# Similarity blocks by symmetry: products on and right of the diagonal, turned copies left of it, three PSUM pairs, and four margins on GpSimd

## The chip, the core and the metric

The kernel runs on one core of a Trainium2 chip. The metric is device time in microseconds (us) of one execution; a kernel's time is the median of several. The engines are TensorE (PE; its weight loads are shown as PEld), VectorE (DVE), ScalarE (ACT), GpSimd (POOL) and SyncE (SP), which issues all DMAs here. Each engine runs its own list of instructions in order, and they meet through semaphores.

## The reference

x is 64 batches of 128 x 1024. From it one graph over the 1024 columns is made, and then every batch is mixed along that graph:

```python
h = relu(layernorm(x))                      # over the 1024 columns
x_avg = h.mean over the 64 batches          # a vector of 128 for each of 1024 nodes
x_norm = x_avg / norm(x_avg)
sim = (x_norm @ x_norm.T + 1) * 0.5         # 1024 x 1024, symmetric
adj = (sim + gumbel0 > 1 - sim + gumbel1)   # not symmetric: gumbel is drawn per entry
adj_sym, nmask = clip(adj + adj.T), with the diagonal set
common = nmask @ nmask.T                    # common neighbours
W = adj * common**2 / common.max()          # where valid
Wn = W scaled by deg**-0.5 on both sides
out = x + (Wn.T applied to h @ weight) + bias
```

The comparison comes down to "x_norm @ x_norm.T is greater than gumbel1 - gumbel0"; the right side is called the margin.

## The kernel before

The work has three parts. First, all 64 batches are loaded once and their statistics and the sum of relu(layernorm) are made (to about 107 us of the trace). Second, the graph is made (about 107 to 235 us): norms of the mean's columns, similarity, comparison, symmetrising, counting of common neighbours, degrees, and the scaled matrix split in two f16 parts. Third, batches go in pairs through x·W and the product with the graph's matrix, in a steady loop that TensorE bounds (235 us to the end).

The change is in the second part. N = 1024 is cut into C = 8 block rows of P = 128. PSUM has 8 banks of 128 x 512 fp32, used as four pairs; a pair holds one 128 x 1024 row.

- **Similarity, TensorE (L750 to L762).** For each block row c, two fp32 products of 128x512 (`xn` chunk c against each half of `xn`) go to `ps_sim[c % 2]`, one of two pairs. From row 2 on TensorE waits until comparison c-2 has read its pair (L752). After rows 2 to 5 come two chunks each of batch 1's x·W (`first_xw`, L742), which need only TensorE. The first row also waits for the two halves of `xn` (L1073).
- **Comparison, VectorE (L1076 to L1081).** `margin_of(c)` (L1027) subtracts the two interleaved gumbel planes of block row c, in place, as soon as its 1 MB block is loaded; `margin_of(0)` to `margin_of(3)` stand ahead of the first comparison, the other four between the comparisons. The comparison reads the PSUM pair and the margin and writes 0 or 1 in f16 to `adjm`, and tells it in `s_adj`.
- **ScalarE (L567 to L585).** It makes z of batch 0, relu of batch 1 for TensorE, two y parts, then waits for all of batch 1's x·W (`z_of(0, 0, 1)`, L579), makes two more y parts, and goes on to the masks (L584).
- **GpSimd.** Its last work before the stage are two powers (L393) that make 1/norm; then it waits until the counting stage (L410).
- **Symmetrising, TensorE (L778 to L798).** For block rows 0 and 1, and then 2 to 7, it adds `adjm`, its turned blocks and the identity in PSUM. Rows 0 and 1 go along with the comparisons: `for k in range(C): wait_ge(s_adj, k + 1)`. Row 0 uses `pair[1]`, row 1 `pair[3]`, which ScalarE must have read (`s_z`), since batch 1's x·W was there.
- **SyncE (L294).** When all eight comparisons are done, it issues six loads of x for the first batches (L300) into the space where the last gumbel block was.

Counting (L831 to L852) already uses a symmetry of the same kind, in f16: products on and right of the diagonal, a copy by ScalarE (`copied`, L562), and turned copies as products with the identity (`mirrored`, L846).

Of the kernel before, what the change touches and what calls it, by code (L numbers as in the profile page):

```python
# [23 lines left out]
ALU = mybir.AluOpType  # L24
ACT = mybir.ActivationFunctionType
# [4 lines left out]
P = 128  # L30
# [7 lines left out]
BODY = 8  # L38
RESIDENT = 0
GUMBEL_SLOTS = 7  # L40
EPS = 1e-5
NORM_MIN = 1e-12
TINY = 1e-30
# [8 lines left out]
def gnn_kernel(nc, x, adj, bias, gumbel, out):  # L52
    B, T, N = x.shape
    C = N // P
    H = 512
# [11 lines left out]
    with ExitStack() as ctx:  # L67
        def sb(name, shape, dt=F32):
            return ctx.enter_context(nc.sbuf_tensor(name, shape, dt))

        def sem(name):
            return ctx.enter_context(nc.semaphore(name))


        xring = sb("xring", [P, BODY, N])
# [7 lines left out]
        ident = sb("ident", [P, P])  # L83
# [39 lines left out]
        adjm = xring[:, 0:4, :].bitcast(F16).rearrange("p a (b n) -> p (a b) n", b=2)  # L123
        nmask = xring[:, 4:8, :].bitcast(F16).rearrange("p a (b n) -> p (a b) n", b=2)
        S, sq, xn = (hring[:, k, :] for k in (2, 1, 3))
        x1 = ([xring[:, k, :] for k in range(8)] + [ybuf[:, k, :] for k in range(7)] + [obuf[:, 0, :]])
        gum7 = a16[:, :, :, :, :].bitcast(F32).rearrange("p k m c n -> p (k m c n)").rearrange(
            "p (r n) -> p r n", r=GUMBEL_SLOTS)
        gum = [gum7[:, k, :] for k in range(GUMBEL_SLOTS)] + [
            obuf[:, 2:4, :].rearrange("p a n -> p (a n)")]  # L130
        g0, g1 = ([g.rearrange("p (d g) -> p g d", g=2)[:, k, :] for g in gum] for k in (0, 1))
        margin = g0
        h1 = [hring[:, k, :] for k in range(4)] + [zbuf[:, k, :] for k in (1, 2, 3)] + [obuf[:, 1, :]]
        acc = zbuf[:, 0, :]
        def tile16(half, mat, k):
            return a16[:, half, mat, 2 * k:2 * k + 2, :].rearrange("p c n -> p (c n)")

        masked = [tile16(half, mat, k) for half, mat in ((0, 5), (1, 5), (1, 3), (1, 4)) for k in (0, 1)]
        count16 = [tile16(c // 4, 1 + c // 2 % 2, c % 2) for c in range(C)]
        squares = a16[:, 0, 0, :, :].bitcast(F32).rearrange("p c n -> p (c n)")  # L140
# [16 lines left out]
        pair = [ps[:, 2 * k:2 * k + 2, :].rearrange("p a n -> p (a n)") for k in range(4)]  # L157
# [2 lines left out]
        ps_w = ps[:, 7, :]  # L160
        ps_norm = [ps[:, 6 + half, 0:HC] for half in (0, 1)]
        ps_bc = pair[1]
        ps_sim = [pair[2], pair[0]]
        ps_sym = [pair[1], pair[3], pair[2], pair[0]]
        ps_com = [pair[1], pair[0]]
        ps_diag = pair[2]
# [11 lines left out]
        s_gum = [sem(f"gumbel_loaded{k}") for k in range(C)]  # L178
# [24 lines left out]
        s_bc = sem("rnorm_row_ready")  # L203
        s_xn = sem("xn_ready")
        s_sim = sem("sim_ready")
        s_margin = sem("margin_ready")
        s_adj = sem("adj_ready")
        s_sym = sem("sym_ready")
        s_mask = [sem(f"nmask_ready{k}") for k in (0, 1)]
# [31 lines left out]
        s_xw2 = sem("xw2_ready")  # L241
# [82 lines left out]
        def _(pool):  # L324

            nc.gpsimd.memset(neg_half[:], -0.5).then_inc(s_pchain, 1)
            nc.gpsimd.memset(eps[:], EPS).then_inc(s_pchain, 1)
            nc.gpsimd.memset(minus_one[:], -1.0).then_inc(s_pchain, 1)
# [61 lines left out]
            for half in (0, 1):  # L390
                cols = slice(half * HC, (half + 1) * HC)
                pool.wait_ge(s_n2s, half + 1)
                nc.gpsimd.tensor_tensor(rnorm[:, cols], norm2[:, cols], neg_half[:, cols], ALU.pow).then_inc(s_rn, 1)  # L393

            def z_sums(r):
                pool.wait_ge(s_z, 2 * r + 2)
                pool.wait_ge(s_y, 4 * r + 4)
                nc.gpsimd.tensor_tensor(z[:, 4, :], z[:, 0, :], z[:, 3, :], ALU.add).then_inc(s_zs, 1)  # L398
                pool.wait_ge(s_zs, 4 * r + 1)
                nc.gpsimd.tensor_tensor(z[:, 5, :], z[:, 4, :], z[:, 1, :], ALU.subtract).then_inc(s_zs, 1)  # L400
                nc.gpsimd.tensor_tensor(z[:, 6, :], z[:, 1, :], z[:, 0, :], ALU.subtract).then_inc(s_zs, 1)  # L401
                pool.wait_ge(s_zs, 4 * r + 2)
                nc.gpsimd.tensor_tensor(z[:, 7, :], z[:, 2, :], z[:, 5, :], ALU.subtract).then_inc(s_zs, 1)  # L403
# [12 lines left out]
            with pool.Fori(2, TRIPS * PAIRS) as r:  # L416
                z_sums(r)

        @block.scalar
        def _(act):  # L420
# [69 lines left out]
            def z_of(i, q, b):  # L490

                i, q = i + q // PAIRS, q % PAIRS
                j, r = 2 * q + b, PAIRS * i + q
                if b == 0:
                    act.wait_ge(s_y, 4 * r + 4)
                if isinstance(i, int) and i == 0 and j == EARLY[1]:
                    src = xw_res[:, 0:1, :].rearrange("p a (m n) -> p (a m) n", m=2)
                elif j == RESIDENT:
                    src = xw_res[:, bass.ds(i, 1), :].rearrange("p a (m n) -> p (a m) n", m=2)
                else:  # L500
                    act.wait_ge(s_xw2, (BODY - 1) * i + j + 2)
                    src = ps_xw2.rearrange("p (m n) -> p m n", m=2)
                dst = z[:, 1:3, :] if b == 0 else z[:, 0:4:3, :]
                nc.scalar.activation(dst, src, ACT.Copy, scale=Y_SCALE / W_SCALE).then_inc(s_z, 1)  # L504

            def y_high_first(u):

                act.wait_ge(s_z, 2 if u >= 2 else 1)
                nc.scalar.activation(y16[:, 0, 0, u, :], z[:, (u + 1) % 4, :], ACT.Copy).then_inc(s_yhi, 1)
# [66 lines left out]
            relu_first(1)  # L576
            y_high_first(0)
            y_high_first(1)
            z_of(0, 0, 1)  # L579
            y_high_first(2)  # L580
            y_high_first(3)
# [43 lines left out]
            for n, (mat, rows, k, half) in enumerate(((0, rows_hi, 0, 0), (A12, rows_hi, 0, 1),  # L625
                                                      (1, rows_lo, 1, 0), (2, rows_lo, 1, 1))):
                for part in (0, 1):
                    a, b = 2 * part, 2 * part + 2
# [43 lines left out]
        def _(pe):  # L672
# [8 lines left out]
                             skip_group_check=True).then_inc(s_wsum, 1)  # L681

            for m in range(2):
                nc.tensor.matmul(ps_avg[:, m * H:m * H + P], zeros[:], ones[:], start=True, stop=True,
                                 skip_group_check=True)
# [44 lines left out]
            for half in (0, 1):  # L730
                pe.wait_ge(s_sq, half + 1)
                for k in range(HC):
                    c = half * HC + k
                    mm = nc.tensor.matmul(ps_norm[half][:, k:k + 1], sq[:, c * P:(c + 1) * P], ones[:, 0:1],
                                          start=True, stop=True, skip_group_check=True)
# [6 lines left out]
            def first_xw(j, chunks):  # L742

                pe.wait_ge(s_fh, EARLY.index(j) + 1)
                for c in chunks:
                    mm = nc.tensor.matmul(ps_xw2[:, c * P:(c + 1) * P], first_h[j][:, c * P:(c + 1) * P], w_unit[:],
                                          start=True, stop=True, skip_group_check=True)
                return mm

            for c in range(C):  # L750
                if c >= 2:
                    pe.wait_ge(s_adj, c - 1)  # L752
                for m in range(2):
                    if c == 0:
                        pe.wait_ge(s_xn, m + 1)
                    mm = nc.tensor.matmul(ps_sim[c % 2][:, m * H:(m + 1) * H], xn[:, c * P:(c + 1) * P],  # L756
                                          xn[:, m * H:(m + 1) * H], start=True, stop=True)
                mm.then_inc(s_sim, 1)
                if 2 <= c < 6:
                    mm = first_xw(1, (2 * c - 4, 2 * c - 3))  # L760
                    if c == 5:
                        mm.then_inc(s_xw2, 1)  # L762

            def sym_start(c):

                for m in (LO, HI):
                    nc.tensor.matmul(ps_sym[c % 4][:, m], ident16[:], adjm[:, c, m], start=True, stop=False,
                                     skip_group_check=True)
                nc.tensor.matmul(ps_sym[c % 4][:, c * P:(c + 1) * P], ident16[:], ident16[:],
                                 start=False, stop=False, skip_group_check=True)  # L770

            def sym_part(c, k):

                return nc.tensor.matmul(ps_sym[c % 4][:, k * P:(k + 1) * P], adjm[:, k, c * P:(c + 1) * P], ident16[:],
                                        start=False, stop=True, skip_group_check=True)


            for k in range(C):  # L778
                pe.wait_ge(s_adj, k + 1)
                if k == 1:  # L780
                    pe.wait_ge(s_z, 2)
                if k < 2:
                    sym_start(k)
                if k == 1:
                    sym_part(0, 0)
                    sym_part(1, 0)
                if k >= 1:
                    for c in (0, 1):
                        mm = sym_part(c, k)
                        if k == C - 1:  # L790
                            mm.then_inc(s_sym, 1)
            for c in range(2, C):
# [3 lines left out]
                for k in range(C):  # L796
                    mm = sym_part(c, k)
# [193 lines left out]
        def _(dve):  # L991
# [35 lines left out]
            def margin_of(c):  # L1027

                dve.wait_ge(s_gum[c], 16)
                nc.vector.tensor_tensor(margin[c], g1[c], g0[c], ALU.subtract).then_inc(s_margin, 1)  # L1030
# [43 lines left out]
                                               op0=ALU.mult, op1=ALU.mult).then_inc(s_xn, 1)  # L1074
            margin_of(3)
            for c in range(C):  # L1076
                if c >= 1 and c + 3 < C:
                    margin_of(c + 3)
                dve.wait_ge(s_sim, c + 1)
                dve.wait_ge(s_margin, c + 1)  # L1080
                nc.vector.tensor_tensor(adjm[:, c, :], ps_sim[c % 2], margin[c], ALU.is_gt).then_inc(s_adj, 1)  # L1081

            def y_low_first(u):
                dve.wait_ge(s_yhi, u + 1)
# [277 lines left out]
```

## Time and profile before

| what | us |
|---|---|
| median of 3 runs | 833.32 |
| lowest, highest | 833.02, 834.04 |
| the profiled execution's own time | 834.8 |
| its span, first to last instruction | 833.1 |
| TensorE busy | 808.6 |
| VectorE, ScalarE, GpSimd busy | 573.0, 495.4, 306.0 |
| start of the first similarity product | 114.46 |
| start of the first symmetrising product | 130.45 |

The profile is of one execution; all stamps are from the span's start. Matmuls overlap: each is shown from its start to its modelled end, so the pitch of a series is read from one start to the next, not from the length of one. An fp32 product is shown as two weight loads and two matmul records, an f16 product as one of each.

### The profile page before, as it was taken

The numbers are of one execution on the slowest core, as the hardware profiler recorded it, in microseconds if no ns is written. First come the engines' busy times: TensorE is split into PE (matmuls) and PEld (weight loads), VectorE is DVE, ScalarE is ACT, GpSimd is POOL, SyncE is SP. The second block draws the span as 40 slices with busy tenths as digits, with TensorE's granted clock in tenths as the row PEclk, the third lists the DMA queues.
The fourth block names the chain that finished last, engine by engine and source line by source line (L and its number), as shares of the span: only waits on it lengthen the run. The fifth ranks groups of instructions, "written<-read, shape, count | busy, mean of one in ns | idle before, by whom it ended". The sixth has DMA issues, their size and how long they took to land.

```text
span 833.1 us, 13478 instructions
## 1 busy us (share of the span) xinstructions
PE 808.6 (97%) x4718; PEld 425.4 (51%) x4718; DVE 573.0 (69%) x687; ACT 495.4 (59%) x515; POOL 306.0 (37%) x257
## 2 busy tenths in 40 slices
PE   4999999999999999999999999999999999999997
PEld 3455465754545554555455545554555455545553
DVE  7999998799976656665666566656665666566652
ACT  3888825588566656665566556656665566556631
POOL 4788810300333334333433343333333333333320
PEclk9999999999999999999999999999999999999999
DMA  8999933000842223222222222222222322232111
GB/s 325 409 410 350 420 131 127 27 1 31 315 160 101 101 102 102 101 101 101 101 101 101 101 101 101 101 101 101 101 101 101 113 99 103 101 116 98 51 51 76
DMA packets 30121, 113.14 MB, mean 136 GB/s; under 512 B 3472, under 2 KB 3600, under 8 KB 29072
## 3 DMA queue, kind: packets, MB, share of 16 engines
q1 hardware_dynamic: 30096, 112.80, 36.6%
q8 instruction: 16, 0.26, 0.1%
q14 instruction: 9, 0.07, 0.0%
HBM read 79.23 MB, written 33.55 MB: 135 GB/s over the span
## 4 chain that ended last, share of the span: by engine, by line
PE 81%; issue 5%; DVE 5%; POOL 4%; ACT 2%; DMA 1%; POOLq 0%; ACTq 0%; SPq 0%; DVEq 0%
PE ps L906 64%; PE ps L823 8%; PE ps L922 2%; POOL rstd L350 2%; PE ps L756 2%; PE ps L841 2%; POOL zbuf L360 1%; DVE stats L1001 1%; PE ps L719 1%; DVE ybuf L1122 1%; DMA xring<-in_x_dram 1%; DVE a L1198 1%; ACT zbuf L430 1%; DVE a L1129 0%; POOL nbias L352 0%
## 5 line engine op out<-in xcount | busy, mean ns | idle before, releaser
L906 PE MATMUL ps<-a,ybuf 128*128 128x512 f16 x2604 | 571.2, 379 | 2.9 <-DVE obuf L1271 1.7
L906 PEld LDWEIGHTS ps<-a,ybuf 128*128 128x128 f16 x2604 | 252.2, 98 | 299.1 <-DVE obuf L1271 2.1
L1122 DVE TENSOR_TENSOR ybuf<-zbuf,ybuf 128x1024 f16<-128x1024 f32 x124 | 166.0, 1340 | 155.3 <-ACT ybuf L523 155.3
L398 POOL TENSOR_TENSOR zbuf<-zbuf 128x512 f32<-128x512 f32 x31 | 39.5, 1275 | 426.8 <-ACT zbuf L504 426.8
L523 ACT ACTIVATE ybuf<-zbuf 128x1024 f16<-128x1024 f32 x124 | 117.6, 950 | 112.6 <-POOL zbuf L403 98.6
L541 ACT ACTIVATE obuf<-ps,bias_sb,w_out 128x512 f32<-128x512 f32 x61 | 47.1, 771 | 113.8 <-PE ps L906 111.5
L1111 DVE TENSOR_TENSOR hring<-hring 128x1024 f16<-128x1024 f32 x53 | 65.4, 1234 | 55.9 <-ACT hring L482 55.8
L823 PEld LDWEIGHTS ps<-w,hring 128*128 128x128 f16 x1272 | 75.4, 98 | 12.4 <-issue 0.4
L1281 DVE TENSOR_TENSOR obuf<-obuf,xring 128x1024 f32<-128x1024 f32 x64 | 78.4, 1225 | 2.7
L823 PE MATMUL ps<-w,hring 128*128 128x128 f16 x1272 | 79.7, 219 | 0.3 <-DVE k L1155 0.3
L504 ACT ACTIVATE zbuf<-ps 128x1024 f32<-128x1024 f32 x55 | 56.3, 1023 | 35.0 <-PE ps L823 20.1
L401 POOL TENSOR_TENSOR zbuf<-zbuf 128x512 f32<-128x512 f32 x31 | 68.2, 2199 | 0.0
L403 POOL TENSOR_TENSOR zbuf<-zbuf 128x512 f32<-128x512 f32 x31 | 67.7, 2184 | 0.0
L472 ACT ACTIVATE hring<-xring,nbias,rstd 128x1024 f32<-128x1024 f32 x49 | 60.2, 1228 | 0.6 <-DMA xring<-in_x_dram 0.6
L482 ACT ACTIVATE hring<-xring,nbias,rstd 128x1024 f16<-128x1024 f32 x49 | 60.1, 1227 | 0.0
L400 POOL TENSOR_TENSOR zbuf<-zbuf 128x512 f32<-128x512 f32 x31 | 49.0, 1580 | 2.4
L1001 DVE BATCH_NORM_STATS2 stats<-xring 128x6 f32<-128x512 f32 x64 | 39.2, 673 | 3.1 <-DMA xring<-in_x_dram 2.8
L719 PE MATMUL ps<-hring,ident 128*128 128x512 f32 x76 | 34.4, 599 | 0.3 <-ACT hring L430 0.3
L1001 DVE BATCH_NORM_STATS2 stats<-ybuf 128x6 f32<-128x512 f32 x56 | 34.0, 668 | 0.0
L719 PE MATMUL ps<-zbuf,ident 128*128 128x512 f32 x60 | 29.6, 632 | 3.0 <-ACT zbuf L430 2.8
L541 ACT ACTIVATE p<-ps,bias_sb,w_out 128x512 f32<-128x512 f32 x31 | 24.0, 773 | 10.4 <-PE ps L906 10.4
L1287 DVE SCALAR_TENSOR_TENSOR obuf<-ps,w_out,obuf 128x512 f32<-128x512 f32 x30 | 22.5, 751 | 9.6 <-PE ps L906 9.5
(142 smaller groups left out, 648.7 us busy)
## 6 DMA issues: line engine op xcount, KB each, us to landing
xring<-in_x_dram SPq DMA_DIRECT2D x96, 512.0 KB, 4.4
out_dram<-obuf SPq DMA_DIRECT2D x64, 512.0 KB, 2.9
ybuf<-in_x_dram SPq DMA_DIRECT2D x28, 512.0 KB, 8.6
a<-in_L_gnn_gumbel_dram SPq DMA_DIRECT2D x7, 1024.0 KB, 15.5
obuf<-in_x_dram SPq DMA_DIRECT2D x11, 512.0 KB, 6.9
obuf<-in_L_gnn_gumbel_dram SPq DMA_DIRECT2D x1, 1024.0 KB, 23.6
w<-in_adj_dram SPq DMA_DIRECT2D x1, 64.0 KB, 1.8
bias_sb<-in_L_gnn_bias_dram SPq DMA_DIRECT2D x1, 0.5 KB, 6.8
```

The costliest lines, as they stand in the source:

```text
L401: nc.gpsimd.tensor_tensor(z[:, 6, :], z[:, 1, :], z[:, 0, :], ALU.subtract).then_inc(s_zs, 1)
L403: nc.gpsimd.tensor_tensor(z[:, 7, :], z[:, 2, :], z[:, 5, :], ALU.subtract).then_inc(s_zs, 1)
L472: nc.scalar.activation(h32, src, ACT.Relu, bias=nbias[:, bass.ds(t, 1)], scale=rstd[:, bass.ds(t, 1)]).then_inc(s_h32, 1)
L523: nc.scalar.activation(y16[:, q % 2, 0, a:a + n, :], z[:, a + 1:a + 1 + n, :], ACT.Copy).then_inc(s_yhi, 1)
L541: nc.scalar.activation(dst, src, ACT.Identity, bias=bias_sb[:, 0:1], scale=w_out[:, 0:1]).then_inc(s_v, 1)
L719: mm = nc.tensor.matmul(ps_avg[:, m], ident[:], h[:, m], start=False, stop=True, skip_group_check=True)
L823: mm = nc.tensor.matmul(ps_xw2[:, c * P:(c + 1) * P], h16[b][:, hk, c * P:(c + 1) * P], w16[:, wk, :], start=(hk == wk == 0), stop=(hk == ...
L906: mm = nc.tensor.matmul(bank[q % 2], y16[:, q % 2, yk, u, c * P:(c + 1) * P], a16[:, ak, mat, c, :], start=(start and c == yk == ak == 0), ...
L1001: nc.vector.bn_stats(stats[:, j % 4, 6 * m:6 * m + 6], x1[j][:, m * H:(m + 1) * H]).then_inc(s_bn, 1)
L1111: nc.vector.tensor_tensor(h16[b][:, 1, :], h32, h16[b][:, 0, :], ALU.subtract).then_inc(s_hlo, 1)
L1122: nc.vector.tensor_tensor(y16[:, q % 2, 1, a:a + n, :], z[:, a + 1:a + 1 + n, :], y16[:, q % 2, 0, a:a + n, :], ALU.subtract).then_inc(s_y, 1)
L1281: nc.vector.tensor_tensor(ob, ob, xring[:, j, :], ALU.add).then_inc(s_out, 1)
```

## The change

TensorE makes only the blocks on and right of the diagonal. ScalarE copies the blocks right of the diagonal of each row from PSUM into SBUF in fp32 (`sim_flat`, which lies in `xring[:, 4:8]`, free at that time), and TensorE turns them (a transpose against the identity) into the rows below. A row is told ready (`s_sim`) after its turned blocks; ScalarE's copy of row c waits for that, and TensorE's turned blocks of row c wait for the copy of row c-1. The rows go through three PSUM pairs, so TensorE waits for comparison c-3. The x·W chunks come one row earlier (rows 1 to 4), ahead of the turned blocks. VectorE's comparison waits for the copy of its row too, and the margins of rows 4 to 7 are made by GpSimd after its two powers. The first symmetrising rows wait for six comparisons at least, since row 0's pair is now used by similarity row 5.

```diff
+POOL_MARGINS = 4
+        sim_flat = xring[:, 4:8, :].rearrange("p a n -> p (a n)")
+        sim_start = [sum(C - 1 - m for m in range(k)) * P for k in range(C)]
+        def sim_copy(k, c):
+            a = sim_start[k] + (c - k - 1) * P
+            return sim_flat[:, a:a + P]
-        ps_sim = [pair[2], pair[0]]
+        ps_sim = [pair[2], pair[0], pair[1]]
 # GpSimd, after the two powers
+            for c in range(C - POOL_MARGINS, C):
+                pool.wait_ge(s_gum[c], 16)
+                nc.gpsimd.tensor_tensor(margin[c], g1[c], g0[c], ALU.subtract).then_inc(s_pmargin, 1)
 # ScalarE, after y_high_first(1)
+            for c in range(C - 1):
+                act.wait_ge(s_sim, c + 1)
+                a = sim_start[c]
+                nc.scalar.activation(sim_flat[:, a:a + (C - 1 - c) * P], ps_sim[c % 3][:, (c + 1) * P:],
+                                     ACT.Copy).then_inc(s_simcopy, 1)
 # TensorE
             for c in range(C):
-                if c >= 2:
-                    pe.wait_ge(s_adj, c - 1)
+                if c >= 3:
+                    pe.wait_ge(s_adj, c - 2)
                 for m in range(2):
                     if c == 0:
                         pe.wait_ge(s_xn, m + 1)
-                    mm = nc.tensor.matmul(ps_sim[c % 2][:, m * H:(m + 1) * H], xn[:, c * P:(c + 1) * P],
-                                          xn[:, m * H:(m + 1) * H], start=True, stop=True)
+                    a, b = max(c * P, m * H), (m + 1) * H
+                    if a < b:
+                        mm = nc.tensor.matmul(ps_sim[c % 3][:, a:b], xn[:, c * P:(c + 1) * P], xn[:, a:b],
+                                              start=True, stop=True, skip_group_check=True)
+                if 1 <= c < 5:
+                    last_xw = first_xw(1, (2 * c - 2, 2 * c - 1))
+                    if c == 4:
+                        last_xw.then_inc(s_xw2, 1)
+                if c >= 1:
+                    pe.wait_ge(s_simcopy, c)
+                for k in range(c):
+                    mm = nc.tensor.transpose(ps_sim[c % 3][:, k * P:(k + 1) * P], sim_copy(k, c), ident[:])
                 mm.then_inc(s_sim, 1)
-                if 2 <= c < 6:
-                    mm = first_xw(1, (2 * c - 4, 2 * c - 3))
-                    if c == 5:
-                        mm.then_inc(s_xw2, 1)
             for k in range(C):
-                pe.wait_ge(s_adj, k + 1)
+                pe.wait_ge(s_adj, max(k + 1, 6))
 # VectorE
             for c in range(C):
-                if c >= 1 and c + 3 < C:
-                    margin_of(c + 3)
                 dve.wait_ge(s_sim, c + 1)
-                dve.wait_ge(s_margin, c + 1)
-                nc.vector.tensor_tensor(adjm[:, c, :], ps_sim[c % 2], margin[c], ALU.is_gt).then_inc(s_adj, 1)
+                if c < C - 1:
+                    dve.wait_ge(s_simcopy, c + 1)
+                if c < C - POOL_MARGINS:
+                    dve.wait_ge(s_margin, c + 1)
+                else:
+                    dve.wait_ge(s_pmargin, c + POOL_MARGINS - C + 1)
+                nc.vector.tensor_tensor(adjm[:, c, :], ps_sim[c % 3], margin[c], ALU.is_gt).then_inc(s_adj, 1)
```

## Rows read from the trace of the kernel before

**Rows 1.** The page: busy time, share and instructions of each engine; the chain that ended last.
```profile
PE 808.6 (97%) x4718; PEld 425.4 (51%) x4718; DVE 573.0 (69%) x687; ACT 495.4 (59%) x515; POOL 306.0 (37%) x257
...
PE 81%; issue 5%; DVE 5%; POOL 4%; ACT 2%; DMA 1%; POOLq 0%; ACTq 0%; SPq 0%; DVEq 0%
```

**Rows 2.** Chain of waits, similarity stage, in order of time: start us, us, what.
```profile
119.96 0.44 PE ps L746 x4
...
127.07 3.54 PE ps L756 x8
...
132.97 0.45 PE ps L774 x8
```

**Rows 3.** Groups by line and form, 114 to 132 us: count, busy us, mean ns, idle.
```profile
L1030 DVE TENSOR_TENSOR a<-a 128x1024 f32<-128x1024 f32 x4 | 4.9, 1217 | 0.0
```

**Rows 4.** Timeline of all engines, 113 to 139 us: start us, us, engine, line, instruction.
```profile
113.53 0.69 DVE L1073 SCALAR_TENSOR_TENSOR hring<-hring,ps 128x512 f32<-128x512 f32 x1 [0.98 <-PE ps L695]
...
114.46 5.50 PE L756 MATMUL ps<-hring 128*128 128x512 f32 x12
...
115.40 0.30 PEld L756 LDWEIGHTS ps<-hring 128*128 128x128 f32 x2 [0.75 <-DVE hring L1073]
...
116.57 1.23 DVE L1081 TENSOR_TENSOR xring<-ps,a 128x1024 f16<-128x1024 f32 x1
...
127.11 1.02 ACT L504 ACTIVATE zbuf<-ps 128x1024 f32<-128x1024 f32 x1 [11.86 <-PE ps L746]
...
127.45 0.19 PEld L756 LDWEIGHTS ps<-hring 128*128 128x128 f32 x1 [0.24 <-issue]
...
130.45 0.59 PE L767 MATMUL ps<-xring,ident 128*128 128x512 f16 x2
...
130.65 1.23 DVE L1081 TENSOR_TENSOR xring<-ps,obuf 128x1024 f16<-128x1024 f32 x1 [0.49 <-PE ps L756]
...
131.90 13.90 SPq L300 DMA_DIRECT2D obuf<-in_x_dram  x6
...
138.20 1.23 ACT L472 ACTIVATE hring<-obuf,nbias,rstd 128x1024 f32<-128x1024 f32 x1
```

**Rows 5.** Timeline, TensorE and ScalarE: fp32 records and counts' copies; one line, L802.
```profile
106.57 1.95 PE L705 MATMUL ps<-w_unit,hring 128*128 128x128 f32 x16
...
141.58 0.92 ACT L564 ACTIVATE a<-ps 128x896 f16<-128x896 f32 x1 [1.02 <-PE ps L841]
...
160.34 0.28 ACT L564 ACTIVATE a<-ps 128x128 f16<-128x128 f32 x1 [0.39 <-PE ps L850]
...
L802 PEld LDWEIGHTS ps<-ident,col x2: 79/82/84, 141.2 to 167.4; 128*1 128x1 f32 x2
L802 PE MATMUL ps<-ident,col x2: 270/271/272, 141.4 to 167.4; 128*1 128x128 f32 x2
```

**Rows 6.** Instructions of one line, GpSimd and VectorE: count, ns min/median/max, first and last start.
```profile
110.29 3.12 POOL L393 TENSOR_TENSOR rnorm<-norm,neg_half 128x4 f32<-128x4 f32 x2 [7.96 <-DVE norm L1066]
...
L360 POOL TENSOR_TENSOR zbuf<-zbuf,hring x11: 2357/2366/2378, 15.4 to 91.8; 128x1024 f32<-128x1024 f32 x11
...
L401 POOL TENSOR_TENSOR zbuf<-zbuf x31: 1263/2301/2310, 155.1 to 803.5; 128x512 f32<-128x512 f32 x31
...
L1122 DVE TENSOR_TENSOR ybuf<-zbuf,ybuf x124: 861/1227/2284, 149.1 to 809.1; 128x1024 f16<-128x1024 f32 x93, 128x512 f16<-128x512 f32 x31
```

**Rows 7.** Stretches: from:to, us, busy PE, PEld, DVE, ACT, POOL, granted clock, DMA share, GB/s.
```profile
23.00:27.00 4.00, 4.00 (x7) 1.61 (x6) 3.73 (x9) 4.00 (x5) 2.35 (x6) 0.57 1.03 410
114.00:117.00 3.00, 3.00 (x12) 1.52 (x11) 2.47 (x4) 1.25 (x3) 0.00 (x0) 1.00 0.02 5
124.00:128.40 4.40, 4.40 (x17) 2.47 (x16) 3.99 (x4) 1.26 (x2) 0.00 (x0) 1.00 0.00 0
```

**Rows 8.** Timeline of TensorE, one row at 22.5 us.
```profile
22.50 2.16 PE L719 MATMUL ps<-zbuf,ident 128*128 128x512 f32 x3 [2.81 <-ACT zbuf L430]
```

More of the change, by code:

```diff
@@ L205, in gnn_kernel @@
         s_sim = sem("sim_ready")
+        s_simcopy = sem("sim_copied")
         s_margin = sem("margin_ready")
+        s_pmargin = sem("margin_by_pool_ready")
         s_adj = sem("adj_ready")
```

## The prediction

> **What bounds the kernel now.** I read the page first: TensorE is busy for 97% of the span and is 81% of the chain that ended last, so a change has to shorten what TensorE does or waits for [rows 1]. The reader is to see there that no other engine can set the end over a long stretch. Then the chain of waits in order of time, around the similarity stage: up to 130.61 us every long piece is TensorE's own, the similarity products (L756) or the eight chunks of the first x·W (L746) put between them, two by two [rows 2]. So this stage, from 114.46 to 130.45 [rows 4], is set by TensorE's work, and VectorE's eight comparisons (L1081, 1.23 us each [rows 4]) and their margins (L1030, 1.22 us each [rows 3]) only just keep up beside it. The timeline by engine gives the stamps: the first comparison starts at 116.57, the symmetrising products (L767) start at 130.45, the last comparison runs from 130.65 to 131.88, ScalarE has nothing to do until 127.11 [rows 4].
>
> **Prices.** A product of 128x512 in fp32 is two records, and their weight loads follow each other at 0.19 + 0.24 = 0.43 us [rows 4], which 3.54 / 8 = 0.44 in the chain confirms [rows 2]; that is 0.1075 us for 128 columns of one record. Sixteen records of 128 columns take 1.95 us with a last one of 0.27, so (1.95 - 0.27) / 15 = 0.11 us each [rows 5]. An fp32 turn (a transpose against the identity) exists in this trace only for a 128x1 column: one load and one matmul record, 0.27 us long [rows 5], as long as one record of an fp32 product. I therefore price a turn of 128x128 at one record, 0.11 us. Ends of this unknown: 0.06 us (an f16 product of 128 columns: 8 of the symmetrising sum take 0.45 us [rows 2]) and 0.22 us (two records, as every fp32 product has).
>
> **The change, part by part.** Of 64 blocks 28 lie left of the diagonal. Their products go: 28 x 2 x 0.1075 = 6.0 us of TensorE. Twenty-eight turns come: 28 x 0.11 = 3.1 us. Were TensorE alone to count, 2.9 us would be gained. But the turns of block row c wait for ScalarE's copy of row c-1, and that copy waits for the turns of row c-1, so the rows are now a chain over two engines, and I walk it.
>
> Nothing changes until row 0 is in PSUM: its second half loads at 115.40, so TensorE is free at 115.40 + 0.11 + 0.86 = 116.37, and row 0 is ready at 116.53. The copies go from PSUM to SBUF; the nearest are the counts' copies, 0.92 us for 896 columns and 0.28 us for 128 [rows 5], so 0.107 us more per block. Those write f16; I take the same for fp32, bounded by a full fp32 row from PSUM at 1.02 us, which lies on the same line (at 1024 columns) [rows 4]. Rows 1 to 4 cost TensorE 7, 6, 5, 4 blocks x 0.215 = 4.73, four pairs of x·W chunks at 0.44 [rows 2] = 1.76, and 1+2+3+4 turns = 1.10 us: TensorE is done with row 4 at 116.37 + 7.59 = 123.96. In this part every copy hides: row 3's, 0.60 us from 122.4, ends at 123.0, and the turns of row 4 start at 123.52 only. The x·W chunks are that cover; without them each of these rows would wait too.
>
> From row 5 on there is no cover. Row 4 is ready at 123.85 + 0.27 = 124.12; its copy takes 0.03 + 0.49, to 124.64; TensorE needs 0.24 us from the end of what released it to its first matmul (VectorE's first half of xn ends at 113.53 + 0.69 = 114.22, the first product starts at 114.46 [rows 4]), so the five turns run from 124.88 to 125.43. Row 6: ready 125.59, copy to 126.01, six turns 126.25 to 126.91. Row 7: ready 127.07, copy to 127.38, seven turns 127.62 to 128.39, and row 7 is ready at 128.55. The products of rows 5 to 7 (0.65, 0.43 and 0.22 us) lie inside these waits. So the symmetrising products start at 128.39 instead of 130.45: **2.06 us earlier**. Of the 2.9 us of work saved 0.8 goes into three waits.
>
> **VectorE.** It loses four margins (4 x 1.22 us) and gains waits for the copies. The first comparison goes from 116.57 to 117.5; behind it are the other seven, and TensorE's row c waits for comparison c-3. They then start at about 119.4, 121.3, 123.0, 124.7, 126.0, 127.4 and 128.6, each after its copy or row: all in time for TensorE, which with three pairs instead of two asks for comparison 0 (done 118.8) only at 120.4. The last ends at 129.8; TensorE wants it after 1.0 us of starts and 14 parts at 0.055, at 130.1. So it hides with 0.3 us to spare. The wait for six comparisons ahead of the first symmetrising product (its PSUM pair is the sixth row's) is met at 127.2, against 128.4.
>
> **ScalarE.** The seven copies stand ahead of its z copy and two y copies. They end at 127.38; the z copy started at 127.11 before [rows 4] and is due when TensorE starts the second symmetrising row, which needs its PSUM pair, at 128.9; it ends at 128.45. Cost nothing, cover 0.4 us.
>
> **GpSimd.** Its four margins come after the two powers, which end at 113.41 [rows 6]; the gumbel blocks are in by then (the DMA engines are 2% busy from 114 to 117 [rows 7]). No row has this operation on GpSimd. The nearest is its add of 128x1024 fp32, 2.37 us beside VectorE's statistics; the far end is 128x512 in 2.30 us, 4.6 us for 1024 [rows 6]. At 2.37 the fourth is done at 122.9, at 4.6 at 131.8; it is due at 128.6, so anything up to 3.8 us each costs nothing. I take 2.4, plus 1 us once where VectorE's last margin (at 115.3) meets them: such pairs show in L401, 1.26 us or 2.30, and in VectorE's L1122, 1.23 us and once 2.28 [rows 6]. If VectorE is the one held up, that margin ends at 117.6 instead of 116.5, when the first comparison is only just due; nothing follows from it. The Trainium skill ("SBUF — State Buffer", the summary's single rule) says that GpSimd and VectorE exclude each other only where VectorE reads two SBUF operands or is in a two-port mode. By it a comparison, which has one operand in PSUM, would slow nothing, so the far end would be out of reach; by plain sharing of the port it would be the case. The trace leans to the rule: 2.37 us beside statistics, which read one operand.
>
> **Behind the stage.** The DMAs of L300 wait for the last comparison and are issued at 131.90, and ScalarE reads the first block at 138.20 with no wait shown [rows 4]; they move 2.1 us earlier with it. From there to the end every start is relative to work before it, and I know of none that stays at its old time. So all 2.06 us arrive: the profiled execution was 834.8 us (span 833.1 and 1.7 around it), 832.7 with the change; against the median of 833.32, which is 1.5 below that execution, **831.3 us**.
>
> **Rivals.**
> 1. *A turn is two records, or its load doesn't hide* (slower). For it: all other fp32 products have two records, and a load alone is 0.19 us long. Against it: the turn of a column has one. Ten turns lie in the TensorE-bound part and 18 in the chain, all on the path, so each 0.01 us more costs 0.28 us, and from 2.06 / 28 = 0.07 us more (0.18 a turn) the kernel is slower. At 0.22: +3.1, that is 834.3.
> 2. *The clock falls.* The trace shows it once: TensorE stood 2.81 us before 22.50 [rows 8], and from 23 to 27 the granted clock averages 0.57 (the 1.2 GHz level for most of it), 4 x 0.43 = 1.7 us of work lost [rows 7]. Here it was at 1.00 and TensorE fully busy [rows 7]; after the change it waits 0.3, 0.4 and 0.5 us in rows 5 to 7. Against it: the waits are short. One such fall takes 1.7 of the 2.06: 833.0. Two: 834.7. The Trainium skill ("TensorE: Matmul & The Clock Gate", Part 4) warns that transposes don't count as activity for the clock. By that TensorE would look mostly idle from 123.5 to 128.4 and this rival would be likely; no row before shows a run of turns.
> 3. *The hand-offs are longer* than 0.24 and 0.03 us, or something behind the stage is not relative. Three rounds are bare; 0.2 us more in each takes 0.6, and the rows before lose their cover last. A gain of 0.5 to 1.5: 832.3.
> 4. *GpSimd's margins are late* (slower). At 4.6 us the last comparison would run from 131.8 to 133.0 against 131.9 before: 834.4. It decides from 4.3 us each on.
> 5. *Turns at the f16 rate* or a better overlap: 28 x 0.05 = 1.4 more: 829.9.
>
> **How the numbers follow.** The forecast 0.55; rival 1 0.10; rival 2 0.10; rival 3 0.14; rival 4 0.03; rival 5 0.08. About 0.2% (1.7 us) is what a measurement can tell from no change, and my gain is only just above it, so a tenth of the forecast's chance falls within it. Faster: 0.49 + 0.08 + 0.01 of the rest = 0.58. Slower by over 0.2% (over 835.0) takes rival 1 above its price, two falls of the clock or the late margins plus something: 0.09, rounded up for what I don't see to 0.12. Within: 0.30. The range runs from rival 5 (829.9, opened to 829.6) to rival 1 (834.3).
>
> **What would show it.** L756's records fall from 32 to 24 (12 products, whole or cut), with 28 turns beside them, one record each, at a pitch of 0.11 us; the copies of 0.92 down to 0.28 us; TensorE waits for ScalarE three times, 0.3 to 0.5 us; the symmetrising products start near 128.4; granted clock 1.00 from 114 to 138; GpSimd's margins near 2.4 us, the last done before 125. Two records a turn, a clock below 1, or a last comparison that waits for GpSimd would each prove me wrong; so would a start at 128.4 with an end that is not 2 us earlier.

## The result, and the profile after

| | before | after |
|---|---|---|
| median of 8 runs each, us | 833.9 | 831.1 |
| ratio of the two, 95% interval | | 0.9972 [0.9963, 0.998] |
| profiled execution, us | 834.8 | 831.14 |
| span | 833.1 | 829.4 |

The kernel is 0.28% faster, 2.3 us with 1.7 to 3.1 as the interval. The forecast was 831.3, a ratio of 0.9976, which lies in the interval; that it is within 0.2 us of the median is closer than the interval can tell. The spans of the two profiles differ by 3.7 us, more than the ratio says. Of these 0.2 come before the stage (the first similarity product starts at 114.46 and at 114.26), 2.43 in it, and 1.05 after it, where the change does nothing; this last part is taken up below.

The page after, the parts of [rows 1]:

```profile
PE 806.0 (97%) x4738; PEld 426.1 (51%) x4738; DVE 567.9 (68%) x683; ACT 499.8 (60%) x522; POOL 317.7 (38%) x261
...
PE 80%; issue 6%; POOL 5%; DVE 4%; ACT 3%; DMA 1%; POOLq 1%; ACTq 0%; SPq 0%; DVEq 0%
```

The chain of waits in the stage after (start us, us, what), against [rows 2]. L777 are the similarity products, L786 the turns, L765 the x·W chunks, L792 the symmetrising products:

```profile
114.42 3.41 PE ps L777 x8
117.83 0.44 PE ps L765 x4
...
123.50 0.44 PE ps L786 x4
...
124.58 0.70 PE ps L786 x5
...
125.75 0.89 PE ps L786 x6
126.67 0.29 ACT xring L596
127.00 0.98 PE ps L786 x7
```

The reader sees the same TensorE pieces as before up to row 4 (its turns from 123.50), then three pieces of turns that each begin with a wait. The timeline of TensorE, and that of its loads, against [rows 4]:

```profile
114.26 3.57 PE L777 MATMUL ps<-hring 128*128 128x512 f32 x8
...
123.33 0.60 PE L786 MATMUL ps<-ident,xring 128*128 128x128 f32 x4
123.77 0.81 PE L777 MATMUL ps<-hring 128*128 128x384 f32 x2
124.52 0.76 PE L786 MATMUL ps<-ident,xring 128*128 128x128 f32 x5
...
127.82 0.59 PE L792 MATMUL ps<-xring,ident 128*128 128x512 f16 x2
```

```profile
124.51 0.53 PEld L786 LDWEIGHTS ps<-ident,xring 128*128 128x128 f32 x5 [0.55 <-ACT xring L596]
...
125.75 0.64 PEld L786 LDWEIGHTS ps<-ident,xring 128*128 128x128 f32 x6 [0.44 <-ACT xring L596]
...
126.99 0.75 PEld L786 LDWEIGHTS ps<-ident,xring 128*128 128x128 f32 x7 [0.33 <-ACT xring L596]
```

The loads of rows 5, 6 and 7 wait 0.55, 0.44 and 0.33 us for ScalarE. Part of that lies under products that TensorE still has to finish: at 0.1075 us a record of 128 columns, the products of row 5 are through at 123.77 + 0.65 = 124.42, and its turns start at 124.52. So TensorE itself loses 0.1, 0.2 and 0.3 us there. The stage, from the first similarity product to the first symmetrising product, lasts 127.82 - 114.26 = **13.56 us**, before 130.45 - 114.46 = **15.99**. The timeline of ScalarE (copies L596, z copy L518), then of VectorE (margin L1055, comparisons L1109):

```profile
116.36 0.92 ACT L596 ACTIVATE xring<-ps 128x896 f32<-128x896 f32 x1 [2.20 <-PE ps L777]
...
123.97 0.49 ACT L596 ACTIVATE xring<-ps 128x384 f32<-128x384 f32 x1 [1.14 <-PE ps L786]
...
126.67 0.28 ACT L596 ACTIVATE xring<-ps 128x128 f32<-128x128 f32 x1 [0.96 <-PE ps L786]
126.84 1.02 ACT L518 ACTIVATE zbuf<-ps 128x1024 f32<-128x1024 f32 x1
```

```profile
115.06 2.94 DVE L1055 TENSOR_TENSOR a<-a 128x1024 f32<-128x1024 f32 x1
117.93 1.23 DVE L1109 TENSOR_TENSOR xring<-ps,a 128x1024 f16<-128x1024 f32 x1
...
128.17 1.22 DVE L1109 TENSOR_TENSOR xring<-ps,obuf 128x1024 f16<-128x1024 f32 x1
```

One line each of the turns (load and product) and of GpSimd's margins (ns min/median/max):

```profile
L786 PEld LDWEIGHTS ps<-ident,xring x28: 138/140/143, 118.0 to 127.6; 128*128 128x128 f32 x28
L786 PE MATMUL ps<-ident,xring x28: 272/273/328, 118.1 to 127.7; 128*128 128x128 f32 x28
```

```profile
L407 POOL TENSOR_TENSOR a<-a x3: 1892/1892/2875, 113.2 to 116.9; 128x1024 f32<-128x1024 f32 x3
L407 POOL TENSOR_TENSOR obuf<-obuf x1: 1888/1888/1888, 119.7 to 119.7; 128x1024 f32<-128x1024 f32 x1
```

The stretch of rows 5 to 7, the same as in [rows 7] and with its columns; the granted clock is 1.00:

```profile
124.00:128.40 4.40, 4.21 (x28) 2.87 (x27) 3.96 (x5) 2.55 (x5) 0.00 (x0) 1.00 0.00 0
```

### The profile page after: what moved, and what is told of

Its sections match the earlier page's. It is cut to its first block, busy times and chain, and to the rows that moved or that the text cites. A ratio compares the mean times of both kernels' runs of the same rounds, so it can differ in the third digit from the quotient of the medians.

```text
span 829.4 us, 13525 instructions
## 1 busy us (share of the span) xinstructions
PE 806.0 (97%) x4738; PEld 426.1 (51%) x4738; DVE 567.9 (68%) x683; ACT 499.8 (60%) x522; POOL 317.7 (38%) x261
## 4 chain that ended last, share of the span: by engine, by line
PE 80%; issue 6%; POOL 5%; DVE 4%; ACT 3%; DMA 1%; POOLq 1%; ACTq 0%; SPq 0%; DVEq 0%
PE ps L931 64%; PE ps L848 8%; PE ps L947 2%; POOL rstd L360 2%; PE ps L866 2%; POOL zbuf L370 1%; PE ps L777 1%; ACT zbuf L444 1%; DVE ybuf L1150 1%; DMA xring<-in_x_dram 1%; POOL nbias L362 1%; DVE a L1226 1%; DVE a L1157 0%; PE ps L786 0%; DVE obuf L1309 0%
## 5 line engine op out<-in xcount | busy, mean ns | idle before, releaser
L1139 DVE TENSOR_TENSOR hring<-hring 128x1024 f16<-128x1024 f32 x53 | 64.9, 1225 | 55.2 <-ACT hring L496 55.1
L518 ACT ACTIVATE zbuf<-ps 128x1024 f32<-128x1024 f32 x55 | 56.3, 1024 | 23.0 <-PE ps L848 20.1
L415 POOL TENSOR_TENSOR zbuf<-zbuf 128x512 f32<-128x512 f32 x31 | 69.2, 2232 | 0.0
L1315 DVE SCALAR_TENSOR_TENSOR obuf<-ps,w_out,obuf 128x512 f32<-128x512 f32 x30 | 22.5, 750 | 9.5 <-PE ps L931 9.4
```

The source lines that it names most:

```text
L1139: nc.vector.tensor_tensor(h16[b][:, 1, :], h32, h16[b][:, 0, :], ALU.subtract).then_inc(s_hlo, 1)
```

## The experiments

"Stage" is always the distance above; "to counting" goes on to the first counting product, so it also holds what a late comparison costs. Each profile gives them to 0.01 us, while a ratio of medians is known to about 0.001 (0.8 us); so the mechanisms are read from the stage, and the ratio says whether the whole agrees.

| kernel | stage | to counting | ratio to before, 95% interval |
|---|---|---|---|
| before | 15.99 | 23.46 | |
| before, second profile (e5) | 15.94 | 23.41 | 1.0004 [0.9995, 1.0013] |
| after | 13.56 | 21.03 | 0.9972 [0.9963, 0.998] |
| after, second profile (e6) | 13.57 | 21.04 | 0.9976 [0.9965, 0.9986] |
| e1 turns as products | 16.89 | 24.37 | 1.0025 [1.001, 1.004] |
| e2 margins on VectorE | 14.59 | 22.57 | 0.9993 [0.9983, 1.0003] |
| e3 full products, helpers kept | 15.71 | 23.18 | 1.0001 [0.999, 1.0012] |
| e4 symmetry, no helpers | 16.00 | 23.47 | 0.9994 [0.9986, 1.0003] |
| e7 x·W later | 13.19 | 20.66 | 0.9964 [0.995, 0.9977] |
| e8 chain over two engines cut | 12.83 | 20.30 | 0.9966 [0.9952, 0.9979] |
| e9 GpSimd waits | 13.56 | 21.03 | 0.996 [0.9946, 0.9975] |
| e10 five margins on GpSimd | 13.56 | 21.03 | 0.9967 [0.9954, 0.998] |

**e1: what a turn costs.**

```diff
-mm = nc.tensor.transpose(ps_sim[c % 3][:, k * P:(k + 1) * P], sim_copy(k, c), ident[:])
+mm = nc.tensor.matmul(ps_sim[c % 3][:, k * P:(k + 1) * P], sim_copy(k, c), ident[:],
+                      start=True, stop=True, skip_group_check=True)
```

> The 28 turns are made as ordinary fp32 products with the identity (two records each) instead of transposes (one record). Theory A, TensorE's work sets the stage and a turn costs one record of 0.11 us: 28 x 0.11 = 3.1 us more, the stage from the first similarity product to the first symmetrising product goes from 13.6 to about 16.6 us and the kernel from 831.1 to about 834.2, slower than before the change. Rival B, the hand-offs between ScalarE and TensorE set the stage: the added records lie inside waits, at most 1 us more, 832.1. Rival C, transposes spare the clock nothing and cost it something, and products keep it up: less than 2 us more.

The turns' line now has twice the records, and each load is longer:

```profile
L786 PEld LDWEIGHTS ps<-ident,xring x56: 186/192/192, 117.4 to 130.3; 128*128 128x128 f32 x56
L786 PE MATMUL ps<-ident,xring x56: 275/275/377, 117.5 to 130.4; 128*128 128x128 f32 x56
```

The stage grows by 3.33 us, 0.119 for each of the 28 added records, and the kernel becomes slower than before. A holds. It also shows that the stage is TensorE's: the added records did not vanish in the waits (B), and the clock gave nothing back (C). This is rival 1 of the prediction, made real: with turns at two records the change would have been a loss.

**e2: the margins back on VectorE.**

```diff
-POOL_MARGINS = 4
+POOL_MARGINS = 0
...
+                if c >= 1 and c + 3 < C:
+                    margin_of(c + 3)
```

> All eight margins on VectorE again, the last four between the comparisons as before the change; symmetry and three pairs stay. Theory A, VectorE has 12 operations of 1.13 us pitch behind the first copy and becomes the bound of the stage's end: the last comparison ends near 131.0 us of the trace instead of 129.4, the third symmetrising row starts 1.5 us later, 832.6. Rival B, TensorE and the hand-offs cover the margins as they did before: 831.1, no change against the changed kernel. In both the one margin that GpSimd's held up (2.9 us long in the changed kernel) is 1.22 us again.

The loads of rows 6 and 7 in TensorE's timeline:

```profile
124.74 0.30 PEld L777 LDWEIGHTS ps<-hring 128*128 128x128 f32 x2 [0.40 <-DVE xring L1111]
...
127.01 0.30 PEld L777 LDWEIGHTS ps<-hring 128*128 128x128 f32 x2 [1.15 <-DVE xring L1111]
```

Before the products of rows 6 and 7 TensorE now waits for comparisons 3 and 4 (L1111), and their turns no longer wait for the copies; 1.54 us are lost to counting against 1.5 expected. A holds: the third pair isn't enough when VectorE itself is the late one.

**e3 and e4: the parts alone.** e3 makes all blocks by products and has no copies and turns; e4 has `ps_sim = [pair[2], pair[0]]`, waits for comparison c-2 and all margins on VectorE.

> All 64 blocks by products, no copies and no turns, but three pairs, the x.W chunks one row earlier and four margins on GpSimd as in the changed kernel. Theory A, the gain is TensorE's work saved by symmetry: the stage is 16 products x 0.86 + 1.76 + 0.2 = 15.7 us, 0.3 less than before, and the kernel 833.6. Rival B, the third pair and the relieved VectorE bring most of the gain: 832 or less.

> Symmetry with two pairs and all margins on VectorE. Theory A, symmetry needs both helpers: TensorE's rows 5 to 7 wait for comparisons 3 to 5, which VectorE's margins push to 125 to 129 us; the first symmetrising product starts near 130, the last comparison ends near 131.4, the kernel is at 833.2, hardly faster than before. Rival B, symmetry carries the gain by itself: 831.3. With the third kernel of this call (helpers without symmetry, 833.6 by A) it tells whether the parts add up or only work together.

Helpers alone gain 0.28 us to counting, symmetry alone loses 0.01, together they gain 2.43. Both expectations by A were met, the stage of e3 to 0.01 us. The 0.28 us of e3 can be seen in TensorE's timeline, two rows of the kernel before and then of e3:

```profile
124.65 1.98 PE L756 MATMUL ps<-hring 128*128 128x512 f32 x4
...
126.91 3.70 PE L756 MATMUL ps<-hring 128*128 128x512 f32 x8
```

```profile
122.22 1.88 PE L772 MATMUL ps<-hring 128*128 128x512 f32 x4
...
124.39 5.32 PE L772 MATMUL ps<-hring 128*128 128x512 f32 x12
```

A row with its x·W chunks takes 2.26 us before (124.65 to 126.91) and 2.17 in e3. VectorE needs 2.27 for a comparison and a margin, so it was already a little late for the old TensorE. So nearly nothing of the gain belongs to symmetry or to the helpers alone: symmetry frees TensorE, and VectorE must be freed with it. Of the two helpers, the third pair brings 0.90 us with the margins still on VectorE (from e4 to e2, to counting), and moving the four margins to GpSimd brings the other 1.54. No run has symmetry and GpSimd's margins with two pairs, so what the margins are worth without the third pair is not shown.

**e5 and e6: the same kernels again.**

> The kernel before, unchanged, for a second profile and for the size of noise. Question: the two profiled executions differ by 3.7 us, of which the stage gives 2.4, the time ahead of it 0.2, and about 1.0 comes between 220 and 234 us, where a load of x takes 6.14 us before and 5.60 after. Theory A, that load and what hangs on it vary from one execution to the next: this profile has a steady loop that starts up to 1 us earlier or later after the stage than 233.63 - 130.45 = 103.18 us, and the ratio of the medians is 1.000. Rival B, the 1.0 us is the change's (an earlier stage meets less traffic): 103.2 again, to 0.2 us.

> The changed kernel, unchanged, for a second profile. Theory A: the stage is 13.56 us to 0.05 (it depends on no DMA), the distance from the first symmetrising product to the steady loop varies around 102.2 us by some tenths; the median is 2.4 below before, a ratio of 0.997. Rival B: the distance is 102.2 to 0.1, always 1 us less than before, and the median is 3.5 below, 0.9958.

The stage repeats to 0.05 us, so it gains 2.4 us in both pairs of profiles. The 1.05 us behind it repeat as well: from the first counting product to the end of the span are 695.18 and 695.41 us in the two profiles of before, 694.11 and 694.19 in the two of after. By that my rival B was right of the profiles. But its median (0.9958) is outside both intervals of the changed kernel, so the medians don't hold the whole of these 1.05 us. The single times of the kernel before fit two values as well: of its 18 runs beside e7, ten took 832.86 to 833.25 us and eight 833.76 to 834.38, though without a profile none of them can be assigned. Over all twelve profiles the distance has two values, 695.1 to 695.5 (before twice, e1, e2, e7) and 694.1 to 694.3 (after twice, e3, e4, e8, e9, e10), without regard to the stage. It arises in one place, the entry to the steady loop: from the loop's first product on all twelve profiles need 599.4 to 599.5 us. First the profile of before: the load of x that ScalarE waits for, from the chain of waits, then VectorE's h_low (L1111) and GpSimd's third z sum (L401) from their timelines:

```profile
222.56 6.14 DMA xring<-in_x_dram
```

```profile
231.21 1.70 DVE L1111 TENSOR_TENSOR hring<-hring 128x1024 f16<-128x1024 f32 x1 [1.08 <-ACT hring L482]
```

```profile
230.56 1.26 POOL L401 TENSOR_TENSOR zbuf<-zbuf 128x512 f32<-128x512 f32 x1
```

The same three in the profile after (h_low is L1139, the sum L415):

```profile
219.93 5.60 DMA xring<-in_x_dram
```

```profile
228.03 1.23 DVE L1139 TENSOR_TENSOR hring<-hring 128x1024 f16<-128x1024 f32 x1 [0.42 <-ACT hring L496]
```

```profile
228.04 2.34 POOL L415 TENSOR_TENSOR zbuf<-zbuf 128x512 f32<-128x512 f32 x1
```

The load lands 0.54 us sooner. Then in before GpSimd has already begun (230.56), and h_low takes 1.70 us instead of 1.23; after, VectorE begins 0.01 us ahead of GpSimd and takes 1.23, and GpSimd takes 2.34. TensorE's first product of the loop starts 0.71 or 0.72 us after the end of h_low in all twelve. In e7 the load took 5.75 us, and h_low the longest of all. VectorE's timeline and GpSimd's:

```profile
227.32 2.35 DVE L1141 TENSOR_TENSOR hring<-hring 128x1024 f16<-128x1024 f32 x1 [0.43 <-ACT hring L497]
```

```profile
227.33 1.26 POOL L416 TENSOR_TENSOR zbuf<-zbuf 128x512 f32<-128x512 f32 x1
```

Here too VectorE begins 0.01 us ahead, and yet it is the one that is held up: with stamps this close, they don't tell which goes first. In the twelve profiles h_low took 1.70 to 2.35 us in just the five that have the long distance, and 1.22 or 1.23 in the seven others. In the five it starts 0.65, 0.64, 0.44 and 0.21 us behind GpSimd's sum and 0.01 ahead of it, and ends each time 2.34 or 2.35 us after that sum's start, as if it stood until the sum is done and then ran for 1.1 us. This is a relation that holds in all twelve, not an intervention: no run here moved the two instructions apart. What decides the landing time stays open.

**e7: which work covers the copies.**

```diff
+XW_ROWS = (2, 3, 5, 6)
...
-                if 1 <= c < 5:
-                    last_xw = first_xw(1, (2 * c - 2, 2 * c - 1))
-                    if c == 4:
+                if c in XW_ROWS:
+                    n = XW_ROWS.index(c)
+                    last_xw = first_xw(1, (2 * n, 2 * n + 1))
+                    if n == 3:
```

> The four pairs of x.W chunks go to rows 2, 3, 5 and 6 instead of 1 to 4. Theory A, in rows 1 to 4 the products alone (1.50 to 0.86 us) cover ScalarE's copy (0.9 to 0.6 us), and the chunks' 0.44 us cover the waits of rows 5 and 6: TensorE's loads wait 0.55 and 0.44 us less there, and the first symmetrising product starts 0.5 to 0.7 us earlier after the first similarity product (13.0 us instead of 13.56); the end gains less if VectorE's last comparison, which then has 0.3 us less to spare, holds it. 830.7. Rival B, as my prediction said, the chunks are the cover of rows 1 to 4: rows 1 and 4 then wait, the stage stays at 13.5 us or grows.

The timeline of TensorE (L778 products, L788 turns):

```profile
113.78 3.57 PE L778 MATMUL ps<-hring 128*128 128x512 f32 x8
117.19 0.27 PE L788 MATMUL ps<-ident,xring 128*128 128x128 f32 x1
...
121.97 0.65 PE L788 MATMUL ps<-ident,xring 128*128 128x128 f32 x4
...
126.15 0.98 PE L788 MATMUL ps<-ident,xring 128*128 128x128 f32 x7
```

Row 1's turn starts at 117.19, as soon as its products are through (their last record starts at 113.78 + 3.57 - 0.59 = 116.76, with 0.59 the length of a 512-column record, and the next can follow 0.43 later), and row 4's at 121.97, without the chunks. So the products do cover the copies of rows 0 and 3, against what I had written. Rows 5 and 6 lose their waits, row 7 keeps its 0.33 us. 0.37 us are gained, less than the 0.5 to 0.7 of A: A had taken the loads' 0.55 and 0.44 us as lost time, while TensorE itself had lost only 0.1 and 0.2 us there.

**e8: the chain cut.**

```diff
# ScalarE: for rows 4 to 6 the copy waits for the products alone
-                act.wait_ge(s_sim, c + 1)
+                if c < HC:
+                    act.wait_ge(s_sim, c + 1)
+                else:
+                    act.wait_ge(s_simprod, c - HC + 1)
# TensorE: HC is 4; turned blocks 0 to 3 go to the bank that the copy doesn't read
+                if HC <= c < C - 1:
+                    mm.then_inc(s_simprod, 1)
...
-                if c >= 1:
+                if 1 <= c <= HC:
                     pe.wait_ge(s_simcopy, c)
                 for k in range(c):
+                    if k == HC:
+                        pe.wait_ge(s_simcopy, min(c + 1, C - 1))
```

> The chain over two engines is cut: from row 4 on, ScalarE's copy waits only for the row's products, and TensorE makes the turned blocks of the lower PSUM bank while the copy reads the upper one; the x.W chunks in rows 2, 3, 5 and 6, five margins on GpSimd. Theory A, no wait of TensorE is left, the stage is its work, 12.8 us plus 0.1, against 13.56; VectorE's comparisons follow each other from row 3 on at a pitch of 1.13 us and their last ends near 128.6; the kernel is 0.7 us faster than the changed one, 830.4. Rival B, VectorE becomes the bound at the end and returns it: first symmetrising product earlier, third symmetrising row not, 831.1.

The kernel also has the x·W chunks of e7 and the five margins of e10. The end of the stage in TensorE's timeline:

```profile
125.37 0.39 PE L782 MATMUL ps<-hring 128*128 128x128 f32 x2
125.59 0.93 PE L796 MATMUL ps<-ident,xring 128*128 128x128 f32 x7
126.36 0.59 PE L802 MATMUL ps<-xring,ident 128*128 128x512 f16 x2
```

Seven turns follow the last product at once. The stage is 12.83 us, 0.73 less, where 12.8 to 12.9 had been expected; symmetrising and counting follow as early, so VectorE returns nothing (B fails). It is the shortest stage of all, but the intervals of its ratio and of the changed kernel's overlap, so that it is faster as a whole is argued from the stage and not shown by the ratio; the same holds for e7. Three changes are in it at once. Against e7, which has the chunks where e8 has them, the stage is 0.36 us shorter, and e10 shows that the fifth margin on GpSimd does nothing to the stage by itself.

**e9 and e10: GpSimd beside VectorE.** e9 adds `pool.wait_ge(s_margin, 4)` ahead of GpSimd's margins; e10 has `POOL_MARGINS = 5` and no `margin_of(3)`.

> GpSimd's four margins wait for VectorE's fourth margin. In the changed kernel VectorE's fourth margin took 2.94 us where the other three took 1.22, beside GpSimd's margins, which took 2.2 and once 1.9 us. Theory A, the two share a read port and the one that starts second stands still until the other's instruction ends: with the wait VectorE's margin takes 1.22 us, the first comparison starts with the end of the first copy (0.65 us earlier relative to the stage), GpSimd's margins take 1.9 us each (no two-operand work of VectorE beside them) and end about 2 us later than before, still ahead of the comparisons; the stage stays 13.56 us and the time the same, since 2 us of VectorE's slack absorbed the stall. Rival B, the 2.94 us are the price of anything beside GpSimd or of memory traffic: it stays above 1.3 us.

> Five margins on GpSimd, three on VectorE, so that no two-operand instruction of VectorE stands beside GpSimd's. Theory A: the first comparison starts at the end of the first copy, the stage stays 13.56 us since TensorE and the hand-offs set it, five margins of 1.9 to 2.2 us end by 124 us, in time; no change of the time against the changed kernel (ratio to before 0.997). Rival B, the late first comparison (0.65 us) does hold TensorE's rows through the pairs: the stage gets up to 0.6 us shorter.

VectorE's margins in e9, all four, and GpSimd's:

```profile
L1056 DVE TENSOR_TENSOR a<-a x4: 1216/1217/1219, 108.3 to 114.8; 128x1024 f32<-128x1024 f32 x4
```

```profile
L408 POOL TENSOR_TENSOR a<-a x3: 1900/1901/1902, 116.1 to 119.8; 128x1024 f32<-128x1024 f32 x3
```

With the wait the fourth margin takes 1.22 us again, and GpSimd's never more than 1.90, though four comparisons run beside them. (The 2.2 us of e9's expectation was misread, the mean of three margins of which one took 2.88; the others took 1.89.) So in the changed kernel VectorE's margin, started at 115.06, must have stood until GpSimd's second ended at 116.9, run 1.1 us, and held GpSimd's third in turn, 2.88 instead of 1.89. The first comparison comes 3.11 us after the first product instead of 3.67, and nothing follows: the stage is 13.56 in e9, in e10 and in the changed kernel. A holds for both.

## Why the prediction was right

- **TensorE's work.** Products at 0.1075 us per 128 columns and record, turns at one record: from the first similarity product to the end of row 4's turns 123.96 - 114.46 = 9.50 us were walked, 123.77 - 114.26 = 9.51 measured. This term carried the forecast.
- **The price of a turn.** One load and one product each, as the column's had. Four in a row take 0.60 us, (0.60 - 0.27) / 3 = 0.11 each. e1 shows the other end, 0.12 more for each.
- **The hand-offs, mis-sized.** Rows 5 to 7 were walked at 4.43 us and took 4.05. I had taken 0.24 us from the releaser's end to the first product, as it was after VectorE; from ScalarE it is 0.06, 0.04 and 0.05 (the first: copy to 124.46, turn at 124.52), 0.57 less in three rounds. Of this 0.15 goes back, since turns that start after a wait take 0.05 us longer than walked (seven of them 0.98, and 0.93 without a wait in e8). That makes the stage's gain 2.43 instead of 2.06. Why the hand-off is shorter from ScalarE is not shown. The other direction, 0.03, was 0.04. The copies were as priced: 0.49 and 0.28 us, fp32 or f16.
- **The waits.** "0.8 goes into three waits" doesn't fit the walk itself, in which TensorE stands for 0.27, 0.39 and 0.49 us, together 1.15; measured were 0.6. The 0.8 came from comparing with the work saved, 2.9, as if the kernel before had lost nothing; it had lost the 0.28 us that e3 gives back.
- **The cover.** Wrong in its reason, harmless for the sum: I wrote that without the x·W chunks rows 1 to 4 would wait too; e7 shows rows 1 and 4 without them and without a wait.
- **VectorE.** Its last comparison was to end at 129.8 and ended at 128.17 + 1.22 = 129.39, in time for TensorE, which went on to the third row without a wait; in e2, with all margins on VectorE, that row comes 1.54 us later. That VectorE "only just keeps up" before was not quite so: e3 shows it late by about 0.1 us in each of three rows. The first comparison was later than I said (117.93 against 117.5).
- **GpSimd.** 2.4 us a margin taken, 1.89 measured; the last ended at 121.6 and was due at 128.17. The far end of 4.6 (rival 4) was never near. The Trainium skill ("SBUF — State Buffer", "Who interferes with whom", where its single rule stands) says that the shared port is an exclusive lock and that work of VectorE with one SBUF input is free of it, other than in the two-port modes. The trace agrees on both: 1.89 us beside comparisons, and beside a two-operand margin both stand in turn, 2.94 and 2.88 us.
- **ScalarE's z copy** started at 126.84, before 127.11: hidden, as forecast.
- **The clock (rival 2).** It stayed at 1.00 from 114 to 138, with waits of at most 0.55 us at the loads. Just ahead of the stage it did fall in two executions: in the second profiles, of before (e5) and of the changed kernel (e6) alike, it is 0.50, the 1.2 GHz level, from 112 to 114 us, though TensorE is shown busy there as in the first profiles, and the stage starts 1.2 us later (115.68 and 115.47 against 114.46 and 114.26). So this fall isn't the change's; inside the stage it stayed at 1.00 in all twelve profiles. The Trainium skill ("TensorE: Matmul & The Clock Gate", Part 4) says that transposes don't count as activity. In 4.4 us with 18 turns and 1.3 us of products the clock did not fall, so here the rule cost nothing; the stretch is short, and a longer run of turns was not tried.
- **Behind the stage.** The 2.63 us by which the symmetrising started earlier are there unchanged at counting (137.92 and 135.29) and at the issue of the x load (222.56 and 219.93): everything was relative, as said. What I did not see is the meeting of VectorE and GpSimd near 228 us, by which one execution is a microsecond shorter or longer than its stage says. The ratio's interval holds both the 2.06 us of the forecast and the 2.43 of the stage and can't choose between them.

## What to carry to other kernels

Walk such a chain instruction by instruction from stamps, with the hand-off latency read from the same pair of engines: that gave the stage's gain as 2.06 against 2.43 measured, where "work saved" alone said 2.9. In size the two miss by about as much, one low and one high; what the walk gave beyond the number were the three waits, whose removal in e8 took 0.73 us off the stage. Before freeing a bound engine by symmetry, look at who was just fast enough for it: here symmetry alone gained nothing and its helpers alone 0.28 us. When two profiles differ by more than the changed stage does, look for a place where two engines start at nearly the same time. A second profile of each kernel repeated the 1.05 us here; only the medians of many executions, and profiles of other variants, showed that it is not bound to the change.

## What the runs showed of the hardware

- An fp32 transpose of 128x128 is one load (0.14 us, against 0.19 in fp32 products) and one matmul record at a pitch of 0.11 us; the same as an fp32 product with the identity is two of each.
- GpSimd's subtraction of two interleaved fp32 planes, 128x1024, takes 1.89 us, less than its add of contiguous tiles of that size, 2.37 us, in the first part of the kernel [rows 6]. Why is open.
- When a VectorE instruction with two SBUF operands meets a series of GpSimd's, both can lose in one meeting: VectorE's took 2.94 instead of 1.22 us and GpSimd's next 2.88 instead of 1.89.
- A run of turns with waits between them (18 in 4.4 us) left the granted clock at 1.00.
